# Message records of two rows in place of four, column blocks padded to 256 slots in place of 512

## What is computed

```python
N, E, D, NEG_SLOPE = 12500, 400000, 128, 0.2

def _spmm(row, col, vals, x):
    msg = vals[:, None] * x[col]
    return jax.ops.segment_sum(msg, row, num_segments=N)

def _layer(x_prev, row, col, vals, W_a, b_a, W_b, b_b):
    h = _spmm(row, col, vals, x_prev)
    z = (h + x_prev) @ W_a.T + b_a + h * x_prev @ W_b.T + b_b
    return jnp.where(z >= 0, z, NEG_SLOPE * z)

x = emb[x_ids]
x1 = _layer(x, row, col, vals, W1_1, b1_1, W1_2, b1_2)
x2 = _layer(x1, row, col, vals, W2_1, b2_1, W2_2, b2_2)
x3 = _layer(x2, row, col, vals, W3_1, b3_1, W3_2, b3_2)
return jnp.concatenate((x, x1, x2, x3), axis=1)
```

## Time and profile before

| what | value |
|---|---|
| median of 3 runs (lowest, highest) | 11,698.34 us (11,696.65 to 11,720.25) |
| the profiled execution, its own time | 11,624.72 us |
| its span, first to last instruction | 11,622.8 us |
| mean granted PE clock | 0.856 |
| PE, DVE busy | 87%, 70% of the span |
| ACT, POOL busy | 38%, 43% |
| message stages, first to last matmul | 865 us each, three |
| row-number DMA, issue to landing | 156.9 us, once |

### The profile page before, as it was taken

The page is one execution under the profiler, slowest core; times in us unless marked ns, Lnnn a source line. Parts: engine busy times, 40 slices in busy tenths (PEclk is TensorE's granted clock), DMA queues, the critical chain, the costliest instruction groups (busy, mean ns, idle before and its releaser), DMA issues.

```text
span 11622.8 us, 237104 instructions
## 1 busy us (share of the span) xinstructions
PE 10098.9 (87%) x72468; PEld 9127.8 (79%) x72469; DVE 8142.5 (70%) x11525; ACT 4411.5 (38%) x13847; POOL 4948.8 (43%) x3315
## 2 busy tenths in 40 slices
PE   6899997689988848998888899988888999888888
PEld 4677776467777738998888889988888899888888
DVE  6877776777777747776666677766666677666666
ACT  0566665046666604652111146631111356411112
POOL 7577776047777710004555500035555200155553
PEclk8666666766666659999999999999999999999999
DMA  2111111011111198997666679986666699966765
GB/s 77 18 4 4 4 4 15 5 3 4 4 4 4 4 26 277 344 337 245 234 239 233 228 236 341 344 272 237 228 239 236 208 339 343 301 235 231 242 234 182
DMA packets 1186659, 1966.58 MB, mean 169 GB/s; under 512 B 455636, under 2 KB 506904, under 8 KB 1185976
## 3 DMA queue, kind: packets, MB, share of 16 engines
q0 software_dynamic: 467360, 1031.62, 30.3%
q1 hardware_dynamic: 719256, 934.47, 27.2%
HBM read 1212.56 MB, written 752.96 MB: 169 GB/s over the span
## 4 chain that ended last, share of the span: by engine, by line
PE 24%; DMA 24%; issue 6%; POOL 4%; ACT 3%; DVE 2%; POOLq 0%; SPq 0%; ACTq 0%; DVEq 0%
PE ps L899 14%; DMA work<-messages,work 12%; DMA messages<-work 12%; PE ps L890 7%; POOL work L508 4%; ACT work L667 2%; DVE work L1262 1%; PE ps L870 1%; PE ps L927 1%; PE ps L907 1%; PE ps L928 1%; ACT work L684 0%; PE ps L917 0%; SPq L585 0%; DVE work L1234 0%
## 5 line engine op out<-in xcount | busy, mean ns | idle before, releaser
L508 POOL DMA_INDIRECT work<-messages,work x1920 | 2321.1, 1209 | 5077.4 <-issue 3533.5
L899 PE MATMUL ps<-work 128*128 128x125 f32 x30720 | 3768.5, 285 | 600.4 <-DVE work L1262 596.8
L899 PEld LDWEIGHTS ps<-work 128*128 128x128 f32 x30720 | 3644.7, 198 | 724.2 <-DVE work L1262 701.1
L483 POOL DMA_INDIRECT sorted_edges<-stage,run_idx x1270 | 2421.6, 1907 | 1453.1 <-DMA sorted_edges<-stage,run_idx 535.3
L1262 DVE TENSOR_TENSOR work<-work,iota_p 128x1000 f32<-128x1000 f32 x1920 | 2298.1, 1197 | 841.1 <-ACT work L684 838.6
L890 PE MATMUL ps<-xb,work 125*128 x21504 | 2457.2, 277 | 155.4 <-DVE work L1234 92.0
L890 PEld LDWEIGHTS ps<-xb,work 125*128 125x128 f32 x21504 | 2422.7, 193 | 189.7 <-issue 188.9
L783 PEld LDWEIGHTS ps<-hT 128*128 128x128 f32 x12700 | 2178.2, 271 | 411.4 <-issue 388.9
L783 PE MATMUL ps<-hT 128*128 128x80 f32 x12700 | 2181.9, 357 | 306.6 <-ACT hT L626 231.6
L667 ACT ACTIVATE work<-ps,work 128x128 f32<-128x128 f32 x5376 | 1511.8, 371 | 1279.1 <-DMA messages<-work 650.8
L684 ACT ACTIVATE work<-work 128x8 f32<-128x8 f32 x1920 | 577.4, 301 | 3693.6 <-DMA work<-messages,work 3693.6
(11 more groups left out here) (200 smaller groups left out, 4109.5 us busy)
## 6 DMA issues: line engine op xcount, KB each, us to landing
messages<-work SPq DMA_DIRECT2D x2688, 256.0 KB, 6.2
work<-slot_cols SPq DMA_DIRECT2D x672, 256.0 KB, 6.0
work<-messages,work POOLq DMA_INDIRECT x1920, 6.0
sorted_edges<-stage,run_idx POOLq DMA_INDIRECT x1270, 3.2
out_x<-xb SPq DMA_DIRECT2D x150, 125.0 KB
work<-lane_places SPq DMA_DIRECT2D x508, 5.5 KB
out_x<-xb SPq DMA_DIRECT2D x4, 1562.5 KB
sorted_edges<-hT SPq DMA_DIRECT2D x4, 906.0 KB
```

The source lines that it names most:

```text
L483: pool.indirect_dma_start(out=sorted_edges[p], out_offset=bass.IndirectOffsetOnAxis(ap=run_idx[:, q, k:k + 1], axis=0), in_=stage[:, q, k ...
L508: pool.indirect_dma_start(out=ck[:, n, :, :].rearrange("p h x -> p (h x)"), out_offset=None, in_=octs, in_offset=bass.IndirectOffsetOnAxis ...
L899: last = t.matmul(part[n], ck[:, n, j // CH, j % CH * D:(j % CH + 1) * D], sel[:, n % SELB, j, :], start=j == 0, stop=j == CHB - 1)
```

## The change

A column block is padded to 256 slots. `CH` goes from 4 to 2 and `GE` from 512 to 256, so the list has 1664 units (half groups), 425,984 slots. Two half groups make a pair (`SUB` = 2, `GW` = 512 slots), which takes the place of a group: one PSUM bank, one buffer, one store. There are 832 pairs and 52 bodies of 16. The two halves of a pair can belong to different column blocks, so PE uses an offset for each half and loads the 32 offsets of a body in two loads of 16, the second ahead of pair 8. A record has two rows and two row numbers (258 numbers, 1032 bytes), so the store of a pair goes to 256 places of 1024 bytes; a gathered piece is four records, 4128 bytes as before. The row-number DMA writes 212,992 pieces of 8 bytes, before 114,688 of 16. `ZC` becomes 241, and the zeroing reads one constant. `GPP` is 13, with 26 turned tables in seven banks.

The core of the diff:

```diff
-CH = 4
+CH = 2
 GE = P * CH
+SUB = 2
+GW = SUB * GE
+PAIRS = GROUPS // SUB
+ABODIES = PAIRS // AU
-ZC = 224
+ZC = -(-N // ABODIES)
...
                 def store_messages(i, last):
                     for n in range(AU):
-                        sp.dma_start(messages[bass.ds(i * (AU * P) + n * P, P), 0:CH * D], msg[:, n % MR, :]).then_inc(msg_stored[n % MR], DMA)
+                        sp.dma_start(messages[bass.ds(i * (AU * SUB * P) + n * (SUB * P), SUB * P), 0:CH * D].rearrange("(u p) x -> p u x", u=SUB),
+                                     msg[:, n % MR, :].rearrange("p (u x) -> p u x", u=SUB)).then_inc(msg_stored[n % MR], DMA)
...
                 with pe.Fori(0, ABODIES) as i:
-                    _, offs = nc.values_load_multi_w_load_instructions(
-                        group_at[0:1, bass.ds(i * AU, AU)], engines=[mybir.EngineType.PE],
-                    for n in range(AU):
-                        for j in range(CH):
-                            last = t.matmul(ps[:, n % PR, j * D:(j + 1) * D], col_hot[:, n % OHR, j * P:(j + 1) * P],
-                                            x_flat[:, bass.ds(offs[n], D)], start=True, stop=True)
+                    for half in range(SUB):
+                        _, offs = nc.values_load_multi_w_load_instructions(
+                            group_at[0:1, bass.ds(i * (AU * SUB) + half * AU, AU)], engines=[mybir.EngineType.PE],
+                        for m in range(AU // SUB):
+                            n = half * (AU // SUB) + m
+                            for j in range(CH * SUB):
+                                last = t.matmul(ps[:, n % PR, j * D:(j + 1) * D], col_hot[:, n % OHR, j * P:(j + 1) * P],
+                                                x_flat[:, bass.ds(offs[m * SUB + j // CH], D)], start=True, stop=True)
...
-                    v.tensor_scalar(hT[:, bass.ds(i * ZC, ZC)].rearrange("p (a z) -> p a z", a=2),
-                                    iota_p[:, 0:ZC // 2][:, None, :].to_broadcast([P, 2, ZC // 2]), 0.0, None, ALU.mult).then_inc(h_zeroed, 1)
+                    v.tensor_scalar(hT[:, bass.ds(i * ZC, ZC)], ones_f[:, 0:1].to_broadcast([P, ZC]), 0.0, None, ALU.mult).then_inc(h_zeroed, 1)
```

More of the change, by code:

```diff
@@ L91 @@
 CQ = 2
-ZC = 224
-assert ABODIES * ZC >= N and ABODIES * ZC == 12544 and TB == 640 and GROUPS % AU == 0 and AU == CB * BATCH and AU % MR == 0
+ZC = -(-N // ABODIES)
+assert ABODIES * ZC >= N and ABODIES * ZC <= 12544 and TB == 640 and PAIRS % AU == 0 and AU == CB * BATCH and AU % MR == 0
 UNITS = [P, GE]
@@ L233, in graph_layers @@
         VN0 = VAL0 + GROUPS * CH
[L234 to L237, removed]
+        val_now = work[:, VN0:VN0 + AU * CH * SUB]
+        CV0 = VN0 + AU * CH * SUB
+        col_row = wu[:, 4 * CV0:4 * CV0 + CB * BATCH * GW].rearrange("c (h x) -> c h x", h=CB)
+        RR0 = CV0 + CB * BATCH * GW // 4
         row_rel = work[:, RR0:RR0 + BU * CHB].rearrange("p (n j) -> p n j", j=CHB)
@@ L498, in _ @@
                 for n in range(MR):
-                    pool.wait_ge(msg_stored[n], la * (GROUPS // MR * DMA) + GROUPS // MR * DMA)
+                    pool.wait_ge(msg_stored[n], la * (PAIRS // MR * DMA) + PAIRS // MR * DMA)
                 pool.wait_ge(slots_stored, DMA)
@@ L643, in _ @@
                     keep_turned(act, s.activation, 1, ACT.Copy)
[L645 to L649, removed]
+            act.wait_ge(vals_turned, VBANKS)
+            for b in range(VBANKS):
+                r0, r1 = b * 4, min(b * 4 + 4, VROWS)
+                s.activation(val_of.rearrange("p (t r) -> p r t", r=VROWS)[:, r0:r1, :],
+                             ps[:, b, 0:(r1 - r0) * DP].rearrange("p (r t) -> p r t", t=DP), ACT.Copy).then_inc(vals_kept, 1)
+            act.wait_ge(vals_kept, VBANKS)
             with act.Fori(0, LAYERS) as la:
@@ L838, in _ @@
             pe.wait_ge(slots_got, DMA)
[L839 to L843, removed]
+            for r in range(VROWS):
+                k, j = r // CH, r % CH
+                last = t.transpose(ps[:, r // 4, r % 4 * DP:(r % 4 + 1) * DP],
+                                   slots_in[:, k * GE:(k + 1) * GE, 1].rearrange("p (m j) -> p j m", j=CH)[:, j, :], ident[:, :])
+                if r % 4 == 3 or r == VROWS - 1:
+                    last.then_inc(vals_turned, 1)
             when_asked()
```

69 lines of the change are left out of this document (35 added, 34 removed).

## The result

The changed kernel takes 12,354.4 us (median, 12,345.2 to 12,359.5) against 11,704.3 of the kernel before beside it: ratio 1.055, 95% interval 1.053 to 1.057. It is slower by 650 us, and far outside the range of 11,615 to 11,880. The profiled execution took 12,345.2 us, its span is 12,343.2 against 11,622.8: 720.4 us more, since the profile of before stood some 80 us under its timed median.

A forecast was written before the change was run, and what follows sets the result against it. The message stage was taken as bound by DMA, PE close behind. Message stages -45 us over three layers, row-number DMA +70, small things -1: +24 on 11,624.7 us profiled, 11,722 us timed with 74 carried over; range 11,615 to 11,880.

The forecast's parts named there:

- The bound: Message stage: DMA binds at 15.45 us a body, with PE 0.35 us a body behind it.
- Fewer groups: Message stages: 52 bodies replace 56; at 15.45 us a body, 803 us, 62 us less a layer.
- Stores in pieces of 1024 bytes: Message-stage stores: two 1024-byte pieces cost 1.063 times one of 2048, so +0.70 us a body, 16.15 us.
- the line: Piece price drawn through 512- and 2048-byte stores: 5.7 ns per piece plus 0.0417 ns per byte, 48.4 ns for 1024 bytes.
- Rival 3: Message-stage stores: fixed price per piece, at worst 21.9 ns; factor 1.247, 946 us a layer, 12,010 us total; chance 0.15.
- Rival 2: Message stage: 1024-byte pieces cost no more per byte, PE becomes the bound; 817 us a layer, 11,623 in all; chance 0.18.
- Two table loads: Message stage: a second offset load before pair 8 costs 0.2 us a body, range 0 to 0.8.
- The row-number DMA: Before first message stage: lands in 292 us, not 157, delaying column loads and first matmul to 4475; +70 us once.
- Rival 1: Row numbers before first message stage: 8-byte pieces cost by bytes or overlap, so stay hidden; 11,652 us; chance 0.12.
- The gather stage: Gather stages: new record layout costs nothing, length kept to 10 us; at most 19 us from the ACT copy.
- The 74 us between profile and timed median: Whole kernel: timed runs stand 74 us above the profiled execution; difference carried over unchanged.

The follow-up runs named there:

- 32-byte version: Changed kernel with records padded to 1056 bytes and row numbers written in 32-byte pieces: 11,542.2 us against 11,641.7 of the kernel before, ratio 0.992.

## Why the prediction was wrong, step by step

*The bound* was read rightly in kind: DMA ended last and PE stood close behind. But the distance of 0.35 us a body took PE's shortest holes, 0.58 us, for its own pace. With pieces at multiples of 64 the kernel before still took 859 us, 0.1 us a body less than 865. After the change the DMA engines are the only bound, and at 32-byte steps PE is.

*Fewer groups* held as a count: 52 bodies. The 62 us a layer that the prediction draws from it came to 39 in the 32-byte version, where PE is the bound (826 in place of 865); in the changed kernel the next step took back much more.

*Stores in pieces of 1024 bytes* is the step that failed: it priced a piece by its size alone. It drew a line through two rows, 512 and 2048 bytes, as if size were the only thing in which they differ. But the 512-byte pieces of the first output begin at multiples of 512, the 2048-byte ones at multiples of 16, and the new ones at multiples of 8. The runs divide the miss of a stage: forecast 850; 889 where the new pieces keep the 16-byte steps of the old ones, so the line was short by 39 us even there; 970 with the 8-byte steps on the same chip, 81 more; 984, 990 and 1057 on the other three. In the sum: +0.70 us a body forecast (and 0.2 for the second load), +4.9 measured in the profile of after. In place of size the runs showed the step of the addresses: where that is 32 or 64 bytes, the line's 48.4 ns a piece is nearly met, 51 and 49 ns on the mean.

*Rival 3* was the nearest: it named the ends at multiples of 8 bytes, and its signs came, the holes inside a body put down to ACT and DVE, which wait for stores. It erred twice. Its cap, the 21.9 ns of a 16-byte piece, was taken for the whole of what can be lost. And it was argued down with the 27 ns of a 512-byte piece that begins at a multiple of 512, a row that says nothing on the others. Its factor also has a slip: (86.7 - 21.9) / 2 + 21.9 is 54.3 ns, so 1.253 and not 1.247, some 3 us a layer more. With its cap unproven, the range should not have stopped half the way to it.

*Rival 2*, that size costs nothing and PE becomes the bound at 817 us, is what happens at 32-byte steps: 826. The Trainium skill (DMA: Bandwidth & Descriptors, "Specifications") puts the least size for line rate at 512 bytes. The traces here agree only where the steps are wide: 1024-byte stores that begin at multiples of 32 ran at 328 GB/s in a stage that PE bounds, those at multiples of 8 at 255 GB/s in one that DMA bounds.

*Two table loads.* Forecast 0.2 us a body in the shadow of DMA; there it can't be told apart. Where PE is the bound there are two holes of 0.51 us, against the 0.58 assumed for rival 2, and the blocks of 64 matmuls take 772.6 / 104 = 7.43 us on the mean against 14.55 / 2. Together that is the 9 us between 817 and 826.

*The row-number DMA* was right as a mechanism and, on three of four chips, in size: forecast 292 us to land and a first matmul at 4475; 285.9, 282.0 and 287.7 us, with 4475.1, 4468.3 and 4473.8, were measured. On the first chip it took 330.4 us, 24.8 ns a piece in place of 21.9, and 4518.4: +113 for the +70 forecast. The same chip was also the slowest with the 8-byte stores. Where a piece of 8 bytes begins matters little: on one chip the DMA took 275.1 us at multiples of 64 (1088-byte records), 279.8 at 16 and 287.8 at 8.

*Rival 1*, a price by bytes, would have made the DMA 146 us; it fell everywhere. The argument against it, that bytes are not what limits this DMA, is borne out by the 32-byte version: 53,248 pieces of 32 bytes took 42.2 us, 12.7 ns a piece, less per piece than one of 8 or 16 bytes.

*The gather stage* kept its length to about 10 us: +2.9, +6.4 and +11.8 with the dense work behind it, and some 3 us a layer more between the last message and the first gather matmul, where the last stores now land later. Together +29 us that the sum had at nothing. The 32-byte version, whose gathered pieces are 2% longer, has 30 too: its stages are 117 us shorter than those of the earlier trace rows, its span 11,535.5 only 87 shorter than the profile of before. Whether the layout costs this isn't shown: the first to the last gather matmul took 1436 to 1457 us in the changed kernel on the four chips, 1440 to 1448 before. The 74 us between profile and timed median, carried over as they were, had no counterpart: the profile of after stood 9 us under its median.

*Left open.* Why the unaligned stores, and the 8-byte row numbers, cost more on one chip than on the others (970 to 1057 us for the same kernel) isn't known: no run here takes the chip's memory apart. How the memory handles a piece that begins off its step, and which pieces make the tail, wasn't seen either; only the price was.

## What to carry to other kernels

When a row of the trace is to price a transfer that it doesn't show, compare where the pieces begin and end, not their size alone: a record that is halved can lose its alignment. Here it was enough to pad the records so that every piece begins and ends at a multiple of 32 bytes, and to use the padding for data that would otherwise be written in pieces of a few bytes. And count the pieces of every small transfer in front of a queue: the next load waits by their number more than by their bytes (212,992 pieces of 8 bytes took 282 to 330 us, 53,248 of 32 bytes, as much data, 42).

## What the hardware showed that was not expected

- Stores of 1024 bytes to memory go by the steps of their addresses: a stage of 970 to 1057 us at multiples of 8, 889 to 897 at 16, 826 at 32 and 64 (where PE is the bound). The price from 16 to 8 is 6.1 to 6.4 ns a piece and engine on the mean, for pieces of 1024 and 2048 bytes alike (the second by profiles not known to be of one chip).
- That price sits in a tail: the median piece took 46 to 48 ns at every step; over 100 ns took 8 to 11% at 8, 4 to 5% at 16, under 0.1% at 32 and 64.
- Not sharing a 64-byte unit with a neighbour gives back only 33 us of at least 164.
- A piece of 32 bytes at a multiple of 32 costs less (12.7 ns) than one of 8 bytes (21 to 25 ns, 20.7 where it begins at a multiple of 64) or 16 bytes (21.9 ns).
- One table load of 32 offsets took 5.0 us in the median, one of 16 took 1.8, and PE's granted clock over the stage fell to 0.90 when the holes grew from half a microsecond at each load to 2 to 5 us.
